# First units of an expert stage: an earlier signal for the row loads, other buffers for four sums, and another order of four small steps

## What is computed

```python
xn = _layernorm(x, axis=-1)
x = x + _L0_attn_ref(xn, ...) + _L0_ffn_ref(xn, ...)

# attention, per batch of 512 tokens
Q = elu(xn @ Wq.T + bq) + 1.0;  K = elu(xn @ Wk.T + bk) + 1.0;  V = xn @ Wv.T + bv
context = (Q @ (K.T @ V)) / (Q @ (K.sum + 1e-06))
out = context @ Wo.T + bo

# feed-forward
combine = _route(x, gate_weight)          # 4 weights per token, 0 elsewhere
up   = jnp.einsum('th,ehi->eti', x, expert_up)
down = jnp.einsum('eti,eih->eth', jax.nn.silu(up), expert_down)
moe_out = jnp.einsum('te,eth->th', combine, down)
shared  = jax.nn.silu(x @ shared_up) @ shared_down
```

## Time and profile before

| | us |
|---|---|
| median of 3 runs | 843.58 (842.2 to 844.42) |
| the profiled execution, its own time | 846.81 |
| its span, first to last instruction | 845.1 |
| POOL busy in the span | 581.7 (69%) |
| PE busy in the span | 744.0 (88%) |
| DVE busy in the span | 698.6 (83%) |

### The profile page before, as it was taken

The page is one execution under the profiler, slowest core; times in us unless marked ns, Lnnn a source line. Parts: engine busy times, 40 slices in busy tenths (PEclk is TensorE's granted clock), DMA queues, the critical chain, the costliest instruction groups (busy, mean ns, idle before and its releaser), DMA issues.

```text
span 845.1 us, 19794 instructions
## 1 busy us (share of the span) xinstructions
PE 744.0 (88%) x5232; PEld 678.8 (80%) x5232; DVE 698.6 (83%) x2401; ACT 572.8 (68%) x1174; POOL 581.7 (69%) x581
## 2 busy tenths in 40 slices
PE   4999999999999999999968798888979897989671
PEld 3899999999999999999857787777778777878661
DVE  5989999999999999999996788778868787878661
ACT  4877778777778777787615687676757676767540
POOL 1056777777677777776776677777777777777753
PEclk9999999999999999999997999999999999999985
DMA  6245544556445544433338999999999999999988
GB/s 178 69 158 202 206 155 166 200 184 216 174 147 198 184 157 147 144 123 117 114 134 275 297 352 309 328 337 333 342 319 319 323 348 325 330 331 338 332 267 271
DMA packets 142317, 199.66 MB, mean 236 GB/s; under 512 B 16752, under 2 KB 117760, under 8 KB 142208
## 3 DMA queue, kind: packets, MB, share of 16 engines
q1 hardware_dynamic: 111152, 113.41, 43.0%
q0 software_dynamic: 28064, 81.93, 25.2%
q10 hardware_dynamic: 2992, 3.06, 1.2%
HBM read 104.19 MB, written 105.04 MB: 248 GB/s over the span
## 4 chain that ended last, share of the span: by engine, by line
PE 46%; DMA 17%; DVE 16%; issue 9%; POOL 6%; SPq 3%; ACT 1%; DVEq 1%; ACTq 0%; POOLq 0%
PE bank_a L319 21%; PE bank_x L319 10%; PE bank_y L319 9%; DMA xn<-rows_by_expert 8%; DMA rows_by_expert<-xn,f_id 7%; DVE xn L1291 3%; POOL rows_by_expert L587 3%; PE bank_a L1495 3%; DMA x_in<-rows_by_expert 3%; DVE hs_l L1304 2%; POOL rows_by_expert L498 2%; PE bank_a L1334 1%; SPq L326 1%; SPq L438 1%; DVE w L1270 1%
## 5 line engine op out<-in xcount | busy, mean ns | idle before, releaser
L587 POOL DMA_INDIRECT rows_by_expert<-xn,f_id x256 | 249.8, 976 | 85.6 <-issue 50.6
L498 POOL DMA_INDIRECT rows_by_expert<-xn,slots_now x192 | 197.2, 1027 | 103.1 <-issue 44.3
L721 ACT CAST xt_h<-bank_a 128x512 fp32r<-128x512 f32 x143 | 84.0, 587 | 68.2 <-PE bank_a L1495 63.2
L1273 DVE TENSOR_TENSOR xt_l<-bank_a,xt_h 128x512 fp32r<-128x512 f32 x143 | 98.1, 686 | 23.9 <-ACT xt_h L721 23.4
L319 PE MATMUL bank_y<-ws,hs_h 128*128 128x256 f32 x512 | 96.4, 286 | 0.5 <-DVE hs_l L1029 0.5
L504 POOL DMA_INDIRECT rows_by_expert<-xn,slots_now x64 | 80.7, 1260 | 17.9 <-issue 14.2
L319 PE MATMUL bank_x<-xt_h,ws 128*128 128x512 f32 x256 | 92.0, 400 | 0.1
L752 ACT ACTIVATE hid<-bank_x 128x256 f32<-128x256 f32 x143 | 55.0, 384 | 53.9 <-PE bank_x L319 44.7
L319 PEld LDWEIGHTS bank_y<-ws,hs_h 128*128 128x128 f32 x512 | 82.6, 192 | 4.0 <-DVE hs_l L1029 0.7
L319 PE MATMUL bank_y<-ws,hs_l 128*128 128x256 f32 x256 | 73.2, 286 | 0.0
L319 PE MATMUL bank_y<-we,hs_h 128*128 x284 | 63.5, 316 | 10.9 <-DVE hs_l L1304 7.1
(11 more groups left out here) (287 smaller groups left out, 2429.6 us busy)
## 6 DMA issues: line engine op xcount, KB each, us to landing
xn<-rows_by_expert SPq DMA_DIRECT2D x204, 272.0 KB, 4.8
x_in<-rows_by_expert SPq DMA_DIRECT2D x71, 272.0 KB
rows_by_expert<-spare SPq DMA_DIRECT2D x22, 544.0 KB, 5.4
x_in<-in_L_attn_x_dram SPq DMA_DIRECT2D x16, 512.0 KB, 4.0
out_dram<-rows_by_expert SPq DMA_DIRECT2D x8, 1024.0 KB, 14.9
rows_by_expert<-xn,f_id POOLq DMA_INDIRECT x286
rows_by_expert<-xn,slots_now POOLq DMA_INDIRECT x256
xn<-rows_by_expert ACTq DMA_DIRECT2D x11, 272.0 KB, 6.6
```

The source lines that it names most:

```text
L498: G.indirect_dma_start(out=half_rows[:, :], in_=xn[:, c % NB, s, 0:RW], in_offset=None, out_offset=bass.IndirectOffsetOnAxis(ap=slots_now[ ...
L587: G.indirect_dma_start(out=half_rows[:, :], in_=f_y[u % YB][:, tile], in_offset=None, out_offset=offset).then_inc(added[u % CLS], 16)
L721: S_.copy(f_h[u % 4], A[u % 2][:, :].rearrange("p (c s t) -> p c s t", c=KD, s=2)).then_inc(fx_hi, 1)
L1273: V.tensor_tensor(f_l[u % 4], A[u % 2][:, :].rearrange("p (c s t) -> p c s t", c=KD, s=2), f_h[u % 4].bitcast(F32), ALU.subtract).then_inc ...
```

## The change

Six edits belong together.

1. PE turns the whole `table` part of the plan first and signals, then the expert numbers. DVE signals `table_ready` behind the copy of the table, and SP waits for that in place of `plan_ready`.
2. `f_y[4]` to `f_y[7]` get homes in `k_f`, `q_f`, `spare` and `x_in`. SP asks for the sums of units 4, 5 and 6 ahead of the rows of unit 7, with no wait for the scatters of the last batch. The rows of unit 8 now wait for them in every case.
3. The little triangle `upto`, which the plan needs, lies elsewhere in `x_in`, and POOL makes it one batch earlier.
4. ACT, DVE and PE read one word of expert numbers ahead of the units, and the other 23 at u = 2.
5. PE makes the down product of unit 0 before it turns the rows of unit 2, and that of unit 1 before the rows of unit 3.
6. POOL's two waits for `fd_done` and `fu_done` begin with unit 10 instead of unit 6.

```diff
-        upto = reused(x_in, (E, E), XB * SUB * D - E * E)
+        upto = reused(x_in, (E, E), (XB - 1) * SUB * D - E * E)
...
-        f_y = [reused(xn, (2, RW), (i + 4) % 8 * 2 * RW) for i in range(YB)]
+        f_y = [reused(xn, (2, RW), (i + 4) * 2 * RW) for i in range(4)]
+        f_y += [reused(k_f, (2, RW)), reused(q_f, (2, RW), KD * S - 2 * RW), reused(spare, (2, RW)),
+                reused(x_in, (2, RW), 4 * 2 * RW)]
...
-            sp.wait_ge(plan_ready, 1)
+            sp.wait_ge(table_ready, 1)
...
+                if u == EARLY:
+                    sp.wait_ge(scattered[(B - 1) % NB], scatters_until(B - 1))
                 sp.dma_start(f_rows[u % RB], unit_rows(row, 0)).then_inc(rows_loaded[u % RB], 16)
 
             def load_sums(u):
-                if u == 4:
-                    sp.wait_ge(scattered[(B - 1) % NB], scatters_until(B - 1))
+                if u == 5:
+                    sp.wait_ge(q_lo, B)
...
+                if u == EARLY - 1:
+                    for v in range(EARLY // 2, EARLY - 1):
+                        load_sums(v)
                 if u < UNITS:
                     load_rows(u)
-                if 0 <= u - (ROWS_AHEAD - SUMS_AHEAD) < SUMS_BY_ACT:
-                    load_sums(u - (ROWS_AHEAD - SUMS_AHEAD))
+                v = u - (ROWS_AHEAD - SUMS_AHEAD)
+                if 0 <= v < EARLY // 2 or EARLY - 1 <= v < SUMS_BY_ACT:
+                    load_sums(v)
...
+                if c == B - 2:
+                    pool.wait_ge(attn_ready, SUB * (B - 2))
+                    G.memset(upto, 1.0).then_inc(const_step, 1)
+                    pool.wait_ge(const_step, 6)
+                    G.affine_select(out=upto, in_=upto, compare_op=ALU.is_ge, fill=0.0, base=0,
...
-                    if u >= 6:
+                    if u >= 10:
                         if tile == 0:
                             pool.wait_ge(fd_done, min(u + 2, UNITS))
...
-            experts = load_experts(mybir.EngineType.Activation)
+            experts = load_experts(mybir.EngineType.Activation, slice(0, 1))
...
             for u in range(UNITS):
+                if u == 2:
+                    experts += load_experts(mybir.EngineType.Activation, slice(1, WORDS))
...
-            V.tensor_copy(table, X[0][0:COLS, 0:UR].rearrange("p (j u) -> p j u", j=2))
+            V.tensor_copy(table, X[0][0:COLS, 0:UR].rearrange("p (j u) -> p j u", j=2)).then_inc(table_ready, 1)
+            dve.wait_ge(plan_turned, 2)
...
                 if u == 1:
+                    unit_down(0)
                     turn_rows(2)
-                    unit_down(0)
+                    unit_down(1)
                     turn_rows(3)
-                    unit_down(1)
```

More of the change, by code:

```diff
@@ L324, in four_from, with load_experts @@
         def four_from(engine, i, u, low, high):
-            if u % 4 == 0:
-                fours[engine, i] = fours.get((engine, i), ())[-4:] + nc.values_load_multi_w_load_instructions(
-                    table[i:i + 1, u // P, u % P:u % P + 4], engines=[engine], min_val=low, max_val=high,
+            first = u - u % 4
+            known = fours.get((engine, i), {})
+            if first not in known:
+                known = {n: four for n, four in known.items() if n == first - 4}
+                known[first] = nc.values_load_multi_w_load_instructions(
+                    table[i:i + 1, u // P, first % P:first % P + 4], engines=[engine], min_val=low, max_val=high,
                     skip_runtime_bounds_check_because="the plan makes every entry, and makes it within these bounds")[1]
-            return fours[engine, i][-4 + u % 4]
-        def load_experts(engine):
+                fours[engine, i] = known
+            return known[first][u % 4]
+        def load_experts(engine, words):
             return nc.values_load_multi_w_load_instructions(
-                packed, engines=[engine], min_val=0, max_val=(1 << 4 * PACK) - 1,
+                packed[:, words], engines=[engine], min_val=0, max_val=(1 << 4 * PACK) - 1,
                 skip_runtime_bounds_check_because="each word holds PACK expert numbers of four bits")[1]
@@ L531, in _ @@
                     scatter_row(last, 5)
[L532 to L536, removed]
-                                    pattern=[[-1, E], [1, E]], channel_multiplier=0).then_inc(consts_made, 1)
                 if c + 1 < B:
@@ L1263, in _ @@
             dve.wait_ge(plan_ready, 1)
-            experts = load_experts(mybir.EngineType.DVE)
+            experts = load_experts(mybir.EngineType.DVE, slice(0, 1))
             def rows_low(u):
@@ L1299, in _ @@
                     sum_up(1)
+                    experts += load_experts(mybir.EngineType.DVE, slice(1, WORDS))
                 if 1 < u and u + 2 < UNITS:
@@ L1480, in _ @@
             pe.wait_ge(silu_done, SH * B)
-            for j in range(2):
-                T_.matmul(X[0][0:COLS, j * P:(j + 1) * P], u_tab[:, j, :], ident[:, :],
-                          start=(j == 0), stop=True, skip_group_check=True)
-                last = T_.matmul(X[1][0:1, j * P:(j + 1) * P], u_tab[:, j, 1:2], ident[:, :],
-                                 start=(j == 0), stop=True, skip_group_check=True)
-            last.then_inc(plan_turned, 1)
+            for bank, columns in ((X[0][0:COLS, :], slice(0, COLS)), (X[1][0:1, :], slice(1, 2))):
+                for j in range(2):
+                    last = T_.matmul(bank[:, j * P:(j + 1) * P], u_tab[:, j, columns], ident[:, :],
+                                     start=(j == 0), stop=True, skip_group_check=True)
+                last.then_inc(plan_turned, 1)
             down(SH * B - 2)
@@ L1499, in _ @@
             pe.wait_ge(plan_ready, 1)
-            experts = load_experts(mybir.EngineType.PE)
+            experts = load_experts(mybir.EngineType.PE, slice(0, 1))
             pe.wait_ge(attn_ready, SUB * B)
@@ L1517, in _ @@
             for u in range(UNITS + 1):
+                if u == 2:
+                    experts += load_experts(mybir.EngineType.PE, slice(1, WORDS))
                 if u < UNITS:
```

5 lines of the change are left out of this document (3 added, 2 removed).

## The result

| | us |
|---|---|
| before, median of 10 runs | 844.82 (842.2 to 845.72) |
| changed, median of 10 runs | 847.55 (844.79 to 850.11) |
| ratio, with its 95% interval | 1.0034 (1.0019 to 1.005) |
| profiled execution of the changed kernel, its own time | 846.87 |
| its span | 845.1 |

The changed kernel is slower by 0.34%, some 2.8 us. The forecast was 839.8 us, which is 3.8 us less than before. So the loss isn't to be read from the ends of the two traces, but from where the first units stand in them.

The account below looks back on a forecast made before the run. POOL's stores were taken to bound the kernel from unit 8 on. POOL reaching unit 10 4.35 us sooner, less 0.5 us for scatters, gives 3.8 us: 843.6 becomes 839.8 us, with 8 in 10 for 838.4 to 843.2.

Parts of the forecast that it names:

- The bound: From unit 8 on, POOL's stores at 2.53 us per unit; moving its place at about unit 10 moves the end equally.
- The rival in which the lead gets lost: From 484 us the DMA engines bound, earlier POOL waits for its stores to land; 843.6 us, chance 0.10.
- a word costs some 0.09 us, and 23 of them 2.1 us: Price of the expert-number read at u = 2, on each of PE, DVE and ACT, ahead of unit 2's up product.
- worth 0: First units: what was won ahead is about spent on the reads, PE at unit 7's turn about where it was.
- up to 1.7 us late: PE's lateness in the first units if the three reads at u = 2 add up instead of lying side by side.
- Rows 7: Rows of unit 7 come when they come now, at 465.75; three loads in front put 0.5 us on the scatters.
- the rival of late rows: Three loads served ahead of scatters, which land 2.7 us later; PE waits before unit 7, low clock; 843.0 us, chance 0.13.
- Rows 12: Before unit 12, PE's second wait stays about 1.2 us, as everything ahead moves with PE; gain behind it 3.3 us.
- PE's wait for rows 8 and the low clock at 470 us: Before unit 8 the 2.39 us wait goes, and the low clock worth 1.06 us; PE gains 3.4 us at unit 9.
- SP's earlier start and the triangle: First rows leave 1.65 us sooner, near 443.7; the triangle's move takes 0.8 us off before the last scatter, none counted.
- the greater gain: Rival: triangle's 0.8 us reaches the scatters and rows 12 land without PE waiting; about 838.0 us, chance 0.12.
- Longer stores from the new places: Rival: POOL's 143 stores from new places take 0.05 us more each, 7.2 us; 847.0 us, chance 0.05.

Follow-up runs that it names:

- other starts: The kernel before with its reads of 24 expert-number words cut in other ways on PE, ACT and DVE; 845.89 us (one run).
- reads and weights only: The kernel before with only expert numbers read four words at a time from multiples of four, and weights loaded at u = 15; 841.86 us, 0.9982.
- late words alone: The kernel before with only the reads of one word ahead of the units and 23 at u = 2; 847.97 us, 1.0047.
- all words first: The changed kernel with all 24 words of expert numbers read ahead of the units on ACT, DVE and PE; 844.22 us, 0.9989.
- later weights: The changed kernel with expert numbers read four words at a time and weights loaded at u = 15 instead of 12; 842.53, again 842.23 us.

## Why the prediction was wrong

**The bound: right up to the last dozen units.** From unit 10 to unit 130 POOL keeps its beat in all versions on the chips of 844 us, and the order of their times is nearly that of POOL's unit 10. The two kernels late by 4.3 and 3.9 us there take 3.1 and 4.4 us longer (the second in one run), the one that is early by 5.0 takes 3.7 less. A single run with other starts doesn't fit (0.65 early, 2.3 longer), but its time is within the spread of before. The rival in which the lead gets lost did not come true on these chips. From unit 10 to unit 130 POOL takes 305.7 to 307.6 us in each of their versions, and the kernel that is 5.01 us ahead at unit 10 is 5.00 ahead at unit 130 (791.27 against 796.27).

The size is looser than the prediction had it. Three quarters of the shift reach the median in that kernel, and with reads and weights only it is less than half (3.93 us early, 1.7 faster). What the prediction left out is the end of the stage: it looked at POOL's waits up to 800 us only and took the last units to follow. But in the kernel before, too, POOL stands still there, for up to 3.3 us at a time (its waits from 800 to 845 us for DVE's sums: total, times, longest):

```profile
POOL rows_by_expert L590 <- DVE xn L1291: 5.8, 2, 3.3
```

From unit 130 to the end the profiles of these versions take anything from 46.4 to 49.1 us, in no order that goes with the edits, and this 2.7 us is as large as the differences in question. What sets it stays open.

**The failed step: "a word costs some 0.09 us, and 23 of them 2.1 us".** The step was in the sum with that price, and with "worth 0" for its effect. The price came from reads that all start at a multiple of four words, and the new read starts at word 1. It takes 6.4 to 8.2 us, three to four times the price. Then the rest of the step fails too. PE doesn't reach unit 7 about where it was, but 3.8 us later (469.55 against 465.75), and unit 8, where the prediction had the gain, 1.6 us later. The late words alone cost 3.1 us by the medians, 4.0 by the ratio. That is more than half of the 6.5 us between forecast (3.8 less) and result (2.7 more); most of the remainder is in rows 7 and 12, below. The bound on this step, "up to 1.7 us late", was made by adding up reads of the same wrong price, so it held no doubt of the price itself. The Trainium skill, page "Runtime: NRT & Kernel Launch", section "Instruction fetch mechanics", gives about 200 ns for each register that a TENSOR_LOAD fills, also in bulk. As an estimate from that figure 23 words take 4.6 us. The loads that the page describes read HBM, and here the words lie in SBUF. The runs don't show that figure: a word took 70 to 160 ns from a multiple of four and 270 to 360 otherwise. It would have been a warning that 0.09 us isn't the only price of a word.

**Rows 7: a second step that failed, and the rival of late rows was real.** The forecast had the rows of unit 7 come "when they come now" and took 0.5 us for the three loads in front. Behind these loads they land 5.0 us after their issue (460.86 to 465.90, all words first), 4.9 and 5.7 us (later weights, first and second run), not 3.5. With the loads behind them it is 3.1. So the term was 1.4 to 2.6 us. The forecast looked for it in the scatters, for which SP waits, and these did not end later: with all words first SP issues rows 7 1.37 us sooner than before (460.86 against 462.23), and yet PE has them 0.15 us later (465.90 against 465.75). So the 0.5 to 1.05 us that were to fall on the scatters did not show, and the delay came behind the issue. The low clock came with the new wait, as the rival said. Its gain, 0.6 us, is near the 0.65 by which the medians differ without edit 4, but that is within the noise of no change.

**Rows 12: too small.** "PE's second wait stays at about 1.2 us": it is 1.9 to 2.4 us in the versions that are free of the long read and load the weights at 12. PE comes earlier, DVE's step that releases the weights less so. SP waits 5.3 to 6.0 us for it there (8.1 in the changed kernel), and loading the weights at 15 takes PE's wait away.

**PE's wait for rows 8 and the low clock at 470 us: right by luck in the changed kernel.** The wait is gone and the clock over 470 to 478 us is 1.00, but because PE itself comes late, by 3.8 us at unit 7 and 1.6 at unit 8. Without the long read rows 8 are in time too (no wait of PE before them with all words first), which is as forecast, but wait and low clock only moved ahead to unit 7. **SP's earlier start and the triangle: right** (443.65 against a forecast of 443.7; last scatter 0.89 us sooner against 0.8, of which nothing was counted). The last scatter is at 452.9 to 454.0 in the versions with the earlier triangle and at 454.0 to 455.0 in those without.

**A sum:** the terms of the greater gain, 4.35, 0.8 and up to 1.2 us, come to 6.35, which would be 837.3 us and not about 838.0. Nothing hung on it.

**Longer stores from the new places: did not happen.** POOL's stores by home, 490 to 800 us, busy us and mean ns of one in the changed kernel:

```profile
L599 POOL DMA_INDIRECT rows_by_expert<-xn,f_id x116 | 113.1, 975 | 36.1 <-issue 24.4 <-DVE f_id L1301 3.7 <-PE bank_y L321 2.3
L599 POOL DMA_INDIRECT rows_by_expert<-spare,f_id x30 | 29.4, 978 | 9.1 <-issue 6.4 <-PE bank_x L321 0.6 <-DMA rows_by_expert<-k_f,f_id 0.6
L599 POOL DMA_INDIRECT rows_by_expert<-q_f,f_id x30 | 29.2, 974 | 9.1 <-issue 4.6 <-DVE f_id L1301 2.1 <-PE bank_a L321 1.2
L599 POOL DMA_INDIRECT rows_by_expert<-x_in,f_id x30 | 28.9, 963 | 9.1 <-issue 4.9 <-PE bank_y L321 1.8 <-DVE f_id L1301 0.9
L599 POOL DMA_INDIRECT rows_by_expert<-k_f,f_id x30 | 28.9, 963 | 9.1 <-issue 4.3 <-DVE f_id L1301 1.8 <-PE bank_a L321 1.2
```

975 ns from `xn` and 963 to 978 from the new ones. The kernel is slower, as this rival had it, but by another mechanism.

## What to carry to other kernels

A read of words into registers holds up all that its engine has to do behind it: of PE's 8.2 us, 7.3 were idle. Before one is moved or cut, its price is to be measured for the very start and length that it will have: here the cut "one word first, the rest later" made PE's 2.1 us into 8.2, and cuts at multiples of four left 0.5 to 0.6 us ahead of the units and five later reads of 0.3 to 0.7. When a signal comes earlier, the first thing to be asked for with it should be what the bound's supplier waits for: three loads that weren't needed yet, put in front of the one that was, took back all of the earlier start that could be seen. And the bound's place is a finer ruler than the end of one trace. The start of POOL's unit 10 came out the same in two profiles of one kernel (486.62 and 486.56), while the stretch behind unit 130 varied by 2.7 us. It has its own noise: the triangle's MEMSET, still in the first stage and ahead of anything that differs, is at 419.78 to 420.93 us in the versions that have it where the kernel before does, so differences under some 1 us at unit 10 say little. The ruler doesn't replace the medians: 1.5 us between two versions at unit 10 (486.56 and 485.02) were 0.4 us between their medians.

## What the runs showed of the hardware

A TENSOR_LOAD of 20 to 24 words of 4 bytes from one partition took 1.4 to 3.8 us if it began at a multiple of four words, and 5.4 to 8.2 us if it began at word 1 (PE, ACT and DVE alike, early or late in the program) or at word 2 (ACT, one read). Within the first kind it varied with time and place: 24 words from word 0 took 1.7 to 3.0 us ahead of the units, and 3.1 to 3.8 us at u = 2. What in the instruction makes the difference was not seen in the trace.

One of the four chips on which the experiments ran took 973.64 us for the same kernel instead of 844, at 256 GB/s over the unit stage instead of 330. The version that gained 0.4% on one chip showed no gain on it (1.0003, 0.9986 to 1.0021).
